# Attention scores on one Trainium2 core: minus the maximum enters through a row of ones in the masked keys

## The chip, the cores and the metric

The kernel runs on one core of one Trainium2 chip. The metric is the device time of one execution in microseconds; the time before is the median of 3 runs, 216.88 us (215.86 to 217.13). A lower time is better.

## What is computed

A block of a Flamingo-like network on 16 tiles of 128 x 256 float32: normalise x along its last axis, cross attention with 8 heads against `ctx` (queries from x, keys and values both `ctx`), then a gated feed-forward part. Cut to what matters:

```python
def _L0_xattn_ref(q, k, v, gamma):        # q: 16 x 128 x 256, k = v = ctx
    qh = q.reshape(B, 8, 16, 256)
    kh = k.reshape(B, 8, 16, 256)
    vh = v.reshape(B, 8, 16, 256)
    qk = jnp.einsum('bhdq,bhdl->bhql', qh, kh) * scale
    sm = jax.nn.softmax(qk, axis=-1)
    ret = jnp.einsum('bhql,bhdl->bhdq', sm, vh)
    return gamma * ret.reshape(B, 128, 256)
...
x = x + jnp.tanh(g_xattn[0]) * _L0_xattn_ref(_layernorm(x), ctx, ctx, gamma)
x = x + jnp.tanh(g_ffn[0]) * _L0_ffn_ref(_layernorm(x), ...)   # silu(gate) * up, then down
```

The weights of the feed-forward part are rounded to float8_e4m3 values first. The softmax is computed with its row maximum subtracted.

## The kernel before

There are 16 batches (`NB`). In a batch the 128 partitions are 8 heads of 16 rows, in 4 row groups of 32 partitions (`NG`); a row group holds two heads (`PAR`). Scores are made twice.

- **s fills** (`scores(n)`): per batch 8, one for each row group g and half t of the queries. A matmul of 32 rows takes the normalised queries `qn` as weights and the masked keys `km` (two copies of the keys, each with the rows of one head of the pair kept) as moving data, and fills a PSUM bank 128 x 512. VectorE takes minus the maximum of each half (`reduce_max`).
- **turn** (`turn(b)`): TensorE transposes the maxima of batch b (split in two bf16 parts by VectorE, `split_max`) and `ctx` into one bank; ScalarE copies the first half to `max_t` (`max_out`) and the second to `v_t` (`v_out`).
- **t fills** (`scores_t(n)`): the scores again, transposed: weights `c_sb`, moving data the masked queries `qm` (512 columns, float32), then two bf16 matmuls of 4 rows add minus the maximum from `max_t`. ScalarE takes the exponential of the bank (`exps`).
- **weighted** (`weighted(b)`): 16 matmuls of `p_t` with `v_t`.

A float32 matmul appears in the trace as two rows, and a full round of four fills in four different row groups runs side by side.

The order on every engine is written out by hand. TensorE first runs s fills 0 to 11, turn(0) and s fills 12 to 14; then, in **block b** (b = 0 to 15, with n = 8b and m = 8b + 15): s(m), t(n), s(m+1), s(m+2), t(n+1) to t(n+4), s(m+3), s(m+4), weighted(b-1), turn(b+1), s(m+5), t(n+5), s(m+6), t(n+6), s(m+7), t(n+7). So the third item of block b, s(m+1), is the first s fill of batch b+2, and the second, t(n), the first t fill of batch b. Each engine's queue is in order: what stands behind a waiting instruction waits too. The PSUM banks go round in a ring of 8.

GpSimd (POOL) makes, in its iteration b: at b = 2, 6 and 10 the reciprocal standard deviations of four batches (`pow_group`); `keys(b+2)`, two instructions for the masked keys; `queries(b+2)`, one for `qn` and two for the masked queries `qm`; then, at b = 2, 3, 5, 6, 7 and 8, `rounded` (two instructions over 128 x 768 for the rounding of weights), at b = 9 and 13 `attention` (two over 128 x 1024), at b = 12 `rstd_chunk(0)` and `norm_apply_first`. `keys(b+2)` waits until the maxima of batch b are taken.

Of the kernel before, what the change touches and what calls it, by code (L numbers as in the profile page):

```python
# [66 lines left out]
def build(nc, x, ctx, g_xattn, g_ffn, gamma, gate_w, up_w, down_w, gate_scale, up_scale, down_scale, out):  # L67
# [7 lines left out]
    with es:  # L75
# [26 lines left out]
        km = sb("km", [P, 2, PAR, L])  # L102
        qn = sb("qn", [P, 2, L])
        qm = sb("qm", [P, 4, PAR, L])
        neg_max = sb("neg_max", [P, 2, FILLS * PAR, 2])
        nm_parts = sb("nm_parts", [P, LT, P], bf16)
        max_t = sb("max_t", [P, 2, L], bf16)
# [777 lines left out]
```

## Time and profile before

| | |
|---|---|
| median of 3 runs | 216.88 us (215.86 to 217.13) |
| the profiled execution | 216.79 us, of which the span on the core 215.0 us |
| busy: TensorE / VectorE / ScalarE / GpSimd | 195.8 / 158.5 / 124.9 / 145.9 us |
| turn(1) ends / turn(15) ends | 22.7 / 124.6 us |
| attention part (blocks 0 to 15) | about 15 to 143 us; then the feed-forward part |

Matmuls are pipelined and their ends are modelled, so a busy TensorE is not one at its peak. In the rows below the engines are PE (TensorE matmul), PEld (its weight loads), DVE (VectorE), ACT (ScalarE), POOL (GpSimd); L715 is line 715 of the kernel before; times are microseconds from the start of the span.

### The profile page before, as it was taken

How to read it: one execution, taken by the hardware profiler on the slowest of the kernel's cores; microseconds unless marked ns; L12 is line 12 of the kernel's file. 1: busy time of each engine (PE TensorE's matmuls, PEld its weight loads, DVE VectorE, ACT ScalarE, POOL GpSimd, SP SyncE). 2: the span in 40 equal slices, each digit the busy share in tenths (PEclk: the TensorE clock that was granted, in tenths of full speed). 3: DMA queues.
4: the chain of work that ended last, by engine and by line, in shares of the span. 5: the costliest groups of instructions: out<-in, count | busy, mean ns of one | idle time of the engine just before them, and what ended most of it. 6: DMA issues, size and time to landing. Idle time of an engine off the chain costs nothing.

```text
span 215.0 us, 4666 instructions
## 1 busy us (share of the span) xinstructions
PE 195.8 (91%) x1760; PEld 117.6 (55%) x1760; DVE 158.5 (74%) x331; ACT 124.9 (58%) x241; POOL 145.9 (68%) x167
## 2 busy tenths in 40 slices
PE   0759999999999999999999988999799999999980
PEld 0225456665665566556655642447466766666670
DVE  3599999998999897679965633056956677674954
ACT  2013657876787578767875853369447545844430
POOL 5992889948999999965799003554554999566430
PEclk9988999999999999999999996999999999999997
DMA  5699601101131231232311412111320002002022
GB/s 181 198 351 386 132 2 52 39 24 41 52 112 58 84 107 38 68 93 64 115 46 51 132 38 82 50 48 53 104 101 0 2 0 98 3 0 98 5 98 98
DMA packets 19783, 17.75 MB, mean 83 GB/s; under 512 B 4016, under 2 KB 19248, under 8 KB 19760
## 3 DMA queue, kind: packets, MB, share of 16 engines
q1 hardware_dynamic: 19760, 17.44, 26.1%
q8 instruction: 14, 0.23, 0.5%
q14 instruction: 9, 0.07, 0.1%
HBM read 11.02 MB, written 6.42 MB: 81 GB/s over the span
## 4 chain that ended last, share of the span: by engine, by line
PE 77%; DVE 11%; issue 3%; ACT 3%; POOL 2%; DMA 1%; POOLq 1%; SPq 0%; DVEq 0%; ACTq 0%
PE ps L715 19%; PE ps L779 17%; PE ps L756 14%; PE ps L727 11%; PE ps L836 8%; DVE neg_max L534 6%; PE ps L730 4%; PE ps L743 1%; PE ps L740 1%; ACT p_t L459 1%; DMA c_sb<-in_ctx 1%; PE ps L766 1%; ACT xn L488 1%; DVE p_t L688 1%; POOLq L75 1%
## 5 line engine op out<-in xcount | busy, mean ns | idle before, releaser
L534 DVE TENSOR_REDUCE neg_max<-ps 128x2 f32<-128x512 f32 x128 | 79.3, 681 | 12.3 <-PE ps L715 12.2
L715 PE MATMUL ps<-km,qn 32*128 32x512 f32 x256 | 74.0, 669 | 8.5 <-POOL qn L342 7.7
L459 ACT ACTIVATE p_t<-ps 128x512 f32<-128x512 f32 x128 | 67.1, 600 | 21.4 <-PE ps L730 19.4
L727 PE MATMUL ps<-qm,c_sb 32*128 32x512 f32 x256 | 73.6, 635 | 1.3 <-ACT p_t L459 1.3
L779 PE MATMUL ps<-w_exp,w_gu 128*128 128x512 f16 x192 | 47.0, 390 | 1.3 <-DVE w_exp L585 1.3
L425 POOL TENSOR_TENSOR f_lo<-fu,f_hi 128x512 fp32r<-128x512 f32 x23 | 29.3, 1277 | 23.7 <-ACT f_hi L477 23.7
L730 PE MATMUL ps<-max_t,sel 4*128 4x256 bf16 x256 | 34.7, 268 | 0.0
L715 PEld LDWEIGHTS ps<-km,qn 32*128 32x128 f32 x256 | 25.2, 197 | 14.5 <-issue 14.1
L650 DVE SCALAR_TENSOR_TENSOR ga<-th,ps 128x512 f32<-128x512 f32 x24 | 16.4, 682 | 22.1 <-ACT th L472 22.1
L756 PE MATMUL ps<-p_t,v_t 128*32 128x256 f32 x512 | 30.9, 382 | 0.4 <-ACT p_t L459 0.4
L730 PEld LDWEIGHTS ps<-max_t,sel 4*128 4x128 bf16 x256 | 18.6, 94 | 22.8 <-issue 20.1
L472 ACT ACTIVATE th<-ps,gs_half 128x512 f32<-128x512 f32 x24 | 16.5, 686 | 24.0 <-PE ps L779 22.4
L727 PEld LDWEIGHTS ps<-qm,c_sb 32*128 32x128 f32 x256 | 26.8, 184 | 6.0 <-issue 3.5
L779 PEld LDWEIGHTS ps<-w_exp,w_gu 128*128 128x128 f16 x192 | 17.5, 100 | 21.8 <-issue 2.5
L836 PE MATMUL ps<-wd,f_hi 128*128 128x256 f32 x96 | 27.8, 324 | 0.7 <-POOL f_lo L425 0.7
L335 POOL TENSOR_SCALAR km<-c_sb,mask 128x256 f32<-128x256 f32 x32 | 14.9, 479 | 14.4 <-DVE neg_max L534 12.6
L836 PE MATMUL ps<-wd,f_lo 128*128 128x256 f32 x96 | 23.8, 281 | 0.0
L756 PEld LDWEIGHTS ps<-p_t,v_t 128*32 128x32 f32 x512 | 15.0, 109 | 13.5 <-ACT p_t L459 5.1
L836 PEld LDWEIGHTS ps<-wd,f_hi 128*128 128x128 f32 x96 | 18.1, 189 | 3.8 <-POOL f_lo L425 1.4
L342 POOL TENSOR_SCALAR qn<-x_sb,mv,rstd 128x256 f32<-128x256 f32 x16 | 19.8, 1236 | 0.2
L655 DVE SCALAR_TENSOR_TENSOR fu<-ps,gus,ga 128x512 f32<-128x512 f32 x24 | 18.0, 751 | 2.5 <-POOL f_lo L425 1.7
L445 ACT CAST max_t<-ps 128x256 bf16<-128x256 f32 x16 | 6.0, 372 | 23.2 <-PE ps L743 23.2
(65 smaller groups left out, 217.8 us busy)
## 6 DMA issues: line engine op xcount, KB each, us to landing
u_scr<-u_sb SPq DMA_DIRECT2D x32, 128.0 KB
u_n<-u_scr SPq DMA_DIRECT2D x16, 128.0 KB
r_n<-r_scr SPq DMA_DIRECT2D x16, 128.0 KB
out_x<-p_t SPq DMA_DIRECT2D x16, 128.0 KB, 1.8
x_sb<-in_x SPq DMA_DIRECT2D x3, 512.0 KB, 8.9
c_sb<-in_ctx SPq DMA_DIRECT2D x3, 512.0 KB, 8.9
w_all<-in_L_ffn_gate_w SPq DMA_DIRECT2D x1, 768.0 KB, 9.2
w_all<-in_L_ffn_up_w SPq DMA_DIRECT2D x1, 768.0 KB, 9.8
```

Source lines behind the costliest of these rows:

```text
L342: nc.gpsimd.tensor_scalar(qn[:, b % 2, :], x_sb[:, b, :], mv[:, b, 0:1], rstd[:, b:b + 1], ALU.subtract, ALU.mult).then_inc(qn_ok, 1)
L425: nc.gpsimd.tensor_tensor(f_lo[:, it, :], fu[:, it % 2, :], f_hi[:, it, :].bitcast(f32), ALU.subtract).then_inc(fl_ok, 1)
L459: nc.scalar.activation(p_t[:, b % 2, i, :], ps[:, bank_of["t", n][0], :], ACT.Exp, scale=DH ** -0.5).then_inc(exp_ok, 1)
L472: nc.scalar.activation(th[:, it % 2, :], ps[:, gate_bank(n, 0), :], ACT.Tanh, scale=gs_half[:, it:it + 1]).then_inc(th_ok, 1)
L534: nc.vector.tensor_reduce(neg_max[:, b % 2, at:at + PAR, 0], ps[:, bank_of["s", n][0], :].rearrange("p (e l) -> p e l", e=PAR), axis=AX.X, ...
L655: nc.vector.scalar_tensor_tensor(fu[:, it % 2, :], ps[:, gate_bank(n, 1), :], gus[:, it:it + 1], ga[:, it % 2, :], ALU.mult, ALU.mult).the ...
L715: nc.tensor.matmul(ps[:, bank, :], qn[rows, b % 2, P * t:P * (t + 1)], km[rows, b % 2].rearrange("p e l -> p (e l)"), start=True, stop=Tru ...
L727: nc.tensor.matmul(ps[:, bank, :], c_sb[rows, b, P * t:P * (t + 1)], qm[rows, b % 4].rearrange("p e l -> p (e l)"), start=True, stop=False)
L730: last = nc.tensor.matmul(ps[:, bank, L * e:L * (e + 1)], sel[head, e, :], max_t[head, b % 2, :], start=False, stop=(e == PAR - 1))
L756: last = nc.tensor.matmul(ps[SLOTW * g:SLOTW * (g + 1), bank, L * e:L * (e + 1)], v_t[:, b % 3, t, PAR * g + e, :], p_t[:, b % 2, i, L * e ...
L779: last = nc.tensor.matmul(ps[:, gate_bank(n, m), :], w[:, ht, P * it:P * (it + 1)], x_t[:, c, part, ht, :], start=(j == 0), stop=(j == 2 * ...
L836: last = nc.tensor.matmul(ps[:, PS_Y + q // 2, L * (q % 2):L * (q % 2 + 1)], f[:, it, P * q:P * (q + 1)], wd[:, it, :], start=(it == 0 and ...
```

## The change

Minus the maximum no longer enters the t fills by matmuls of its own.

- `km` is built as keys x mask + `one`, where `one` holds 1 in the first row of the other head of the pair; it has 4 buffers instead of 2 and is now also the weight of the t fills, whose `c_sb` matmul of 512 columns and two bf16 matmuls of 256 become two float32 matmuls of 256 columns.
- The maxima stay float32: `split_max` is gone, `reduce_max` writes into `nm`, and `turn` transposes that.
- `max_out` is two ScalarE instructions, one for each head of the pair, with the mask as scale.
- `queries` makes `qn` only. A new GpSimd step, `shifted_queries(b)`, adds `qn` and `max_t` to give `qm`; it waits for `max_out(b)`. In GpSimd's iteration b it is done for batch b+1, behind `keys(b+2)` and `queries(b+2)` and ahead of `rounded`.
- Subtracting the mean becomes adding its negative (`neg_m`, one small instruction for each group of batches).
- The second instruction of `binades` moves from VectorE to GpSimd, into `rounded`.

```diff
@@ gpsimd
             def keys(b):
-                pool.wait_ge(masks_ok, 1)
+                pool.wait_ge(masks_ok, 3)
                 pool.wait_ge(c_in[group_of(b)], 16)
-                if b >= 2:
-                    pool.wait_ge(max_ok, FILLS * (b - 1))
-                for e in range(PAR):
-                    nc.gpsimd.tensor_scalar(km[:, b % 2, e, :], c_sb[:, b, :], mask[:, e:e + 1], 1.0,
-                                            ALU.mult, ALU.mult).then_inc(k_ok, 1)
+                if b >= 4:
+                    pool.wait_ge(exp_ok, FILLS * (b - 3))
+                for s in range(PAR):
+                    nc.gpsimd.tensor_scalar(km[:, b % 4, s, :], c_sb[:, b, :], mask[:, 1 - s:2 - s], one[:, s:s + 1],
+                                            ALU.mult, ALU.add).then_inc(k_ok, 1)
 
             def queries(b):
                 pool.wait_ge(r1_ok, group_of(b) + 1)
...
+                nc.gpsimd.tensor_scalar(qn[:, b % 3, :], x_sb[:, b, :], neg_m[:, b:b + 1], rstd[:, b:b + 1],
+                                        ALU.add, ALU.mult).then_inc(qn_ok, 1)
+
+            def shifted_queries(b):
+                pool.wait_ge(mt_sb, PAR * (b + 1))
                 if b >= 2:
-                    pool.wait_ge(max_ok, FILLS * (b - 1))
-                nc.gpsimd.tensor_scalar(qn[:, b % 2, :], x_sb[:, b, :], mv[:, b, 0:1], rstd[:, b:b + 1],
-                                        ALU.subtract, ALU.mult).then_inc(qn_ok, 1)
-                if b >= 4:
-                    pool.wait_ge(exp_ok, FILLS * (b - 3))
+                    pool.wait_ge(exp_ok, FILLS * (b - 1))
                 pool.wait_ge(qn_ok, b + 1)
-                for e in range(PAR):
-                    nc.gpsimd.tensor_scalar(qm[:, b % 4, e, :], qn[:, b % 2, :], mask[:, e:e + 1], 1.0,
-                                            ALU.mult, ALU.mult).then_inc(qm_ok, 1)
+                q = qn[:, b % 3, :].rearrange("p (a l) -> p a l", a=1).broadcast_to([P, PAR, L])
+                nc.gpsimd.tensor_tensor(qm[:, b % 2], max_t[:, b % 2], q, ALU.add).then_inc(qm_ok, PAR)
...
                 pool.wait_ge(w_exp_ok, k + 1)
+                nc.gpsimd.tensor_scalar(exp, exp, E4M3_MIN_EXP, E4M3_MAGIC, ALU.max, ALU.mult).then_inc(w_mag, 1)
+                pool.wait_ge(w_mag, k + 1)
                 nc.gpsimd.tensor_tensor(raw, raw, exp, ALU.add).then_inc(w_sum, 1)
...
+            shifted_queries(0)
             for b in range(NB):
                 if b + 2 < NB:
                     if b + 2 in (2, 4, 8, 12) and group_of(b + 2) > 1:
                         pow_group(group_of(b + 2))
                     keys(b + 2)
                     queries(b + 2)
+                if b + 1 < NB:
+                    shifted_queries(b + 1)
                 if b in HALF_ROUNDED:
                     rounded(HALF_ROUNDED.index(b))
@@ scalar
             def max_out(b):
                 act.wait_ge(m_ok, b + 1)
                 if b >= 2:
-                    act.wait_ge(exp_ok, FILLS * (b - 1))
-                nc.scalar.copy(max_t[:, b % 2, :], ps[:, bank_of["T", b][0], 0:L]).then_inc(mt_sb, 1)
+                    act.wait_ge(qm_ok, PAR * (b - 1))
+                for e in range(PAR):
+                    nc.scalar.activation(max_t[:, b % 2, e, :], ps[:, bank_of["T", b][0], 0:L], ACT.Copy,
+                                         scale=mask[:, 1 - e:2 - e]).then_inc(mt_sb, 1)
@@ tensor
             def scores_t(n):
                 b, i = divmod(n, FILLS)
                 t, g = i // NG, (i + ASIDE) % NG
                 if i == 0:
-                    pe.wait_ge(mt_sb, b + 1)
                     pe.wait_ge(qm_ok, PAR * (b + 1))
                 bank, held = bank_of["t", n]
                 bank_free(held)
-                rows, head = slice(SLOTW * g, SLOTW * (g + 1)), slice(SLOTW * g, SLOTW * g + ROWS)
-                nc.tensor.matmul(ps[:, bank, :], c_sb[rows, b, P * t:P * (t + 1)],
-                                 qm[rows, b % 4].rearrange("p e l -> p (e l)"), start=True, stop=False)
+                rows = slice(SLOTW * g, SLOTW * (g + 1))
                 for e in range(PAR):
-                    last = nc.tensor.matmul(ps[:, bank, L * e:L * (e + 1)], sel[head, e, :], max_t[head, b % 2, :],
-                                            start=False, stop=(e == PAR - 1))
+                    last = nc.tensor.matmul(ps[:, bank, L * e:L * (e + 1)], km[rows, b % 4, 1 - e, P * t:P * (t + 1)],
+                                            qm[rows, b % 2, e, :], start=True, stop=True)
                 last.then_inc(st_ok[g], 1)
```

On GpSimd, in iteration 3 of the kernel before (keys and queries of batch 5, then the second half-matrix of the rounding), every instruction works for a batch that TensorE reaches later:

```order
L335 TENSOR_SCALAR km<-c_sb,mask 128x256 [waits max_ok,c_in2,masks_ok]
L335 TENSOR_SCALAR km<-c_sb,mask 128x256
L342 TENSOR_SCALAR qn<-x_sb,mv,rstd 128x256 [waits max_ok,r1_ok]
L348 TENSOR_SCALAR qm<-qn,mask 128x256 [waits qn_ok,exp_ok]
L348 TENSOR_SCALAR qm<-qn,mask 128x256
L367 TENSOR_TENSOR w_all<-w_all,w_exp 128x768 [waits w_exp_ok]
L369 TENSOR_TENSOR w_gu<-w_all,w_exp 128x768 [waits w_sum]
```

The same place in the changed kernel, from the shifted queries of batch 3 through `rounded` to the shifted queries of batch 4:

```order
L346 TENSOR_TENSOR qm<-max_t,qn 128x512 [waits exp_ok,qn_ok,mt_sb]
L363 TENSOR_SCALAR w_exp<-w_exp 128x768 [waits w_exp_ok]
L365 TENSOR_TENSOR w_all<-w_all,w_exp 128x768 [waits w_mag]
L367 TENSOR_TENSOR w_gu<-w_all,w_exp 128x768 [waits w_sum]
L330 TENSOR_SCALAR km<-c_sb,mask,one 128x256 [waits exp_ok,c_in2,masks_ok]
L330 TENSOR_SCALAR km<-c_sb,mask,one 128x256
L337 TENSOR_SCALAR qn<-x_sb,neg_m,rstd 128x256 [waits qm_ok,r1_ok]
L346 TENSOR_TENSOR qm<-max_t,qn 128x512 [waits exp_ok,qn_ok,mt_sb]
```

The masked queries have moved behind a wait for ScalarE's `max_t` (`mt_sb`), and the rounding and the next keys and queries stand behind that.

On TensorE, the start of block 2 of the kernel before, from block 2's first fill on:

```order
L715 MATMUL ps<-km,qn 128x512 [waits u_ok]
L727 MATMUL ps<-qm,c_sb 128x512 [waits mt_sb,vt_sb,qm_ok]
L730 MATMUL ps<-max_t,sel 128x256 x2
L715 MATMUL ps<-km,qn 128x512 [waits max_ok,qn_ok,k_ok]
L715 MATMUL ps<-km,qn 128x512 [waits exp_ok]
```

The same place in the changed kernel:

```order
L695 MATMUL ps<-km,qn 128x512 [waits u_ok]
L707 MATMUL ps<-qm,km 128x256 [waits vt_sb,mt_sb,qm_ok]
L707 MATMUL ps<-qm,km 128x256
L695 MATMUL ps<-km,qn 128x512 [waits max_ok,qn_ok,k_ok]
L695 MATMUL ps<-km,qn 128x512 [waits exp_ok]
```

The order of TensorE is the same; the first t fill of a batch still waits for `qm_ok`, and the s fill right behind it for `k_ok` and `qn_ok` of the batch two further on.

## Rows read from the trace of the kernel before

**Rows 1.** The page's chain that ended last, share of the span by engine.

```profile
PE 77%; DVE 11%; issue 3%; ACT 3%; POOL 2%; DMA 1%; POOLq 1%; SPq 0%; DVEq 0%; ACTq 0%
```

**Rows 2.** One 8 us window: length, busy PE, PEld, DVE, ACT, POOL, clock.

```profile
52.00:60.00 8.00, 8.00 (x94) 4.83 (x94) 7.42 (x15) 6.01 (x14) 7.65 (x8) 1.00 0.13 39
```

**Rows 3.** Timeline of PE over block 4: start us, length us, line, operation.

```profile
58.85 0.39 PE L743 MATMUL ps<-ident,c_sb 128*128 128x128 f32 x2
59.16 0.69 PE L715 MATMUL ps<-km,qn 32*128 32x512 f32 x1
...
60.14 0.69 PE L727 MATMUL ps<-qm,c_sb 32*128 32x512 f32 x1
...
60.35 0.80 PE L715 MATMUL ps<-km,qn 32*128 32x512 f32 x2
60.67 0.67 PE L727 MATMUL ps<-qm,c_sb 32*128 32x512 f32 x2
...
63.92 1.93 PE L756 MATMUL ps<-p_t,v_t 128*32 128x256 f32 x32
...
65.91 0.39 PE L743 MATMUL ps<-ident,c_sb 128*128 128x128 f32 x2
```

**Rows 4.** Timeline of ACT behind the turn of 58.85: start, length, line.

```profile
59.27 0.37 ACT L445 CAST max_t<-ps 128x256 bf16<-128x256 f32 x1 [1.22 <-PE ps L743]
59.54 0.40 ACT L452 COPY v_t<-ps 128x256 f32<-128x256 f32 x1
```

**Rows 5.** Groups by line and form: busy us, mean ns, idle before.

```profile
L342 POOL TENSOR_SCALAR qn<-x_sb,mv,rstd 128x256 f32<-128x256 f32 x16 | 19.8, 1236 | 0.2
L335 POOL TENSOR_SCALAR km<-c_sb,mask 128x256 f32<-128x256 f32 x32 | 14.9, 479 | 14.4 <-DVE neg_max L534 12.6 <-DMA c_sb<-in_ctx 1.5
L488 ACT ACTIVATE xn<-x_sb,shift,rstd 128x256 f32<-128x256 f32 x12 | 6.2, 592 | 1.1 <-POOL shift L388 1.1
L727 PEld LDWEIGHTS ps<-qm,c_sb 32*128 32x128 f32 x256 | 26.8, 184 | 6.0 <-issue 3.5 <-ACT p_t L459 1.1 <-DVE neg_max L534 0.6
```

**Rows 6.** Timelines of ACT and POOL, late in the attention part.

```profile
141.62 0.62 ACT L477 CAST f_hi<-fu 128x512 fp32r<-128x512 f32 x1
142.32 1.28 POOL L425 TENSOR_TENSOR f_lo<-fu,f_hi 128x512 fp32r<-128x512 f32 x1 [0.94 <-ACT f_hi L477]
```

**Rows 7.** Timelines of POOL and PE at the first s fill.

```profile
5.59 1.23 POOL L342 TENSOR_SCALAR qn<-x_sb,mv,rstd 128x256 f32<-128x256 f32 x1
6.97 3.79 PE L715 MATMUL ps<-km,qn 32*128 32x512 f32 x16 [6.97 <-POOL qn L342]
```

**Rows 8.** Timeline of POOL: pow_group, keys, rounded, keys; and an attention step.

```profile
56.46 0.24 POOL L325 TENSOR_SCALAR veps<-mv 128x4 f32<-128x4 f32 x1
...
57.91 0.93 POOL L335 TENSOR_SCALAR km<-c_sb,mask 128x256 f32<-128x256 f32 x2
...
61.41 1.80 POOL L367 TENSOR_TENSOR w_all<-w_all,w_exp 128x768 f32<-128x768 f32 x1
...
65.10 0.94 POOL L335 TENSOR_SCALAR km<-c_sb,mask 128x256 f32<-128x256 f32 x2
...
82.20 2.35 POOL L375 TENSOR_TENSOR u_n<-u_n,r_n 128x1024 f32<-128x1024 f32 x1
```

**Rows 9.** Windows of 2 us around a fall of the clock (columns as Rows 2).

```profile
126.00:128.00 2.00, 1.29 (x11) 0.98 (x12) 1.09 (x1) 1.43 (x3) 0.00 (x0) 1.00 0.15 37
132.00:134.00 2.00, 2.00 (x6) 0.60 (x4) 0.00 (x0) 0.00 (x0) 0.92 (x2) 0.50 0.36 119
```

**Rows 10.** Timeline of PE: eight matmuls at the lower and at the full clock.

```profile
130.85 3.53 PE L779 MATMUL ps<-w_exp,w_gu 128*128 128x512 f16 x8
...
138.75 1.90 PE L779 MATMUL ps<-w_exp,w_gu 128*128 128x512 f16 x8
```

**Rows 11.** Timeline of PE: the last matmuls of turn(1) and of turn(15).

```profile
22.29 0.39 PE L743 MATMUL ps<-ident,c_sb 128*128 128x128 f32 x2
...
124.16 0.39 PE L743 MATMUL ps<-ident,c_sb 128*128 128x128 f32 x2
```

More of the change, by code:

```diff
@@ L18 @@
 STEP = "stssttttssPTststst"
-ROWS = 4
 SLOTW = 32
@@ L99, in build @@
         c_sb = sb("c_sb", [P, NB, L])
[L102 to L107, printed above, removed]
+        km = sb("km", [P, 4, PAR, L])
+        qn = sb("qn", [P, 3, L])
+        qm = sb("qm", [P, 2, PAR, L])
+        nm = sb("nm", [P, 2, LT, P])
+        max_t = sb("max_t", [P, 2, PAR, L])
         p_t = sb("p_t", [P, 2, FILLS, PAR * L])
@@ L119, in build @@
         mv = sb("mv", [P, NB, 2])
+        neg_m = sb("neg_m", [P, NB])
         veps = sb("veps", [P, NB])
@@ L324, in pow_group @@
                 pool.wait_ge(ag1_ok, hi)
+                nc.gpsimd.tensor_scalar(neg_m[:, lo:hi], mv[:, lo:hi, 0], -1.0, None, ALU.mult)
                 nc.gpsimd.tensor_scalar(veps[:, lo:hi], mv[:, lo:hi, 1], EPS, None, ALU.add).then_inc(v1_ok, 1)
@@ L392, in norm_apply_first @@
                     q = t
-                    nc.gpsimd.tensor_scalar(xn2[:, q, :], x_sb[:, t, :], mv2[:, t, 0:1], rstd2[:, t:t + 1],
-                                            ALU.subtract, ALU.mult).then_inc(n2_ok, 1)
+                    nc.gpsimd.tensor_scalar(xn2[:, q, :], x_sb[:, t, :], neg_m2[:, t:t + 1], rstd2[:, t:t + 1],
+                                            ALU.add, ALU.mult).then_inc(n2_ok, 1)
+            shifted_queries(0)
             for b in range(NB):
@@ L532, in reduce_max @@
                 v.wait_ge(s_ok[g], n // NG + 1)
-                at = PAR * (NG * t + g)
-                nc.vector.tensor_reduce(neg_max[:, b % 2, at:at + PAR, 0],
+                if b >= 2:
+                    v.wait_ge(m_ok, b - 1)
+                to = nm[:, b % 2, t, :].rearrange("p (g s r) -> p g s r", g=NG, s=PAR)
+                nc.vector.tensor_reduce(to[:, g, :, 0],
                                         ps[:, bank_of["s", n][0], :].rearrange("p (e l) -> p e l", e=PAR),
                                         axis=AX.X, op=ALU.max, negate=True).then_inc(max_ok, 1)
-            def split_max(b):
-                v.wait_ge(max_ok, FILLS * (b + 1))
-                v.wait_ge(consts, 6)
-                if b:
-                    v.wait_ge(m_ok, b)
-                parts = nm_parts[:].rearrange("p t (g r) -> p (t g) r", g=NG)
-                high, low = (parts[:, :, r:ROWS:2] for r in range(2))
-                pair = neg_max[:, b % 2].rearrange("p (m e) r -> p m e r", e=PAR)
-                with nc.allow_low_precision(reason="the two bf16 parts add up to the float32 maximum"):
-                    nc.vector.tensor_reduce(high, pair[:, :, :, 0:1], axis=AX.X, op=ALU.max).then_inc(mx_hi, 1)
-                v.wait_ge(mx_hi, 2 * b + 1)
-                nc.vector.tensor_reduce(pair[:, :, :, 1], parts[:, :, 0:ROWS].rearrange("p m (e r) -> p m e r", r=2)[:, :, :, 0:1],
-                                        axis=AX.X, op=ALU.max, negate=True).then_inc(mx_hi, 1)
-                v.wait_ge(mx_hi, 2 * b + 2)
-                with nc.allow_low_precision(reason="the two bf16 parts add up to the float32 maximum"):
-                    nc.vector.tensor_reduce(low, pair, axis=AX.X, op=ALU.add).then_inc(mx_ok, 1)
             def binades(k):
@@ L714, in scores @@
                 rows = slice(SLOTW * g, SLOTW * (g + 1))
[L715 to L716 removed]
+                nc.tensor.matmul(ps[:, bank, :], qn[rows, b % 3, P * t:P * (t + 1)],
+                                 km[rows, b % 4].rearrange("p e l -> p (e l)"), start=True, stop=True).then_inc(s_ok[g], 1)
             def scores_t(n):
```

58 lines of the change are left out of this document (20 added, 38 removed).

## The prediction

> **What bounds the kernel now.** I read first the chain that ended last [rows 1]: TensorE has 77% of it, no other engine above 11%. Then the windows of the attention part: in [rows 2] TensorE is busy the whole 8 us, VectorE 7.42, GpSimd 7.65, ScalarE 6.01. Then one block in the timeline of TensorE [rows 3]: the last matmuls of one turn start at 58.85, those of the next at 65.91, so a block takes 7.06 us, and nothing in it stands still for long. GpSimd is nearly as full, but it works ahead: its keys and masked queries are for a batch that TensorE reaches a block later, so nobody waits for it. What the reader should take from this: before, the only thing between a turn and the t fills that need it is one ScalarE copy of 0.37 us [rows 4], and that is hidden: the first t fill of the new batch can start only when the round before it has passed its row group, at about 60.7 (the row of 60.67 holds two), 1.5 us behind the end of the turn (58.85 + 0.39 = 59.24).
>
> **What the change takes off TensorE.** The two bf16 matmuls of a t fill. A row group with an s fill hands over after 60.14 - 59.16 = 0.98 us [rows 3], one with a t fill at 60.35, 0.2 later. The new t fill has the same float32 columns in four shorter rows instead of two. A short row of 256 columns costs 1.93 / 8 = 0.24 us in `weighted` (32 rows in 8 rounds of four), so a t fill is 4 x 0.24 = 0.96: I take 0.98, like an s fill. Two t fills for each row group and block: 0.4 us less work a block, 6 us over 15 blocks, if TensorE stayed the bound. VectorE loses `split_max` and half of `binades`: it waits for TensorE already, so that gives nothing beyond the first blocks.
>
> **What it adds: a serial chain.** Two waits matter, and they follow from the two orders. In block b+1 the t fill of batch b+1 needs `shifted_queries(b+1)`, which needs turn(b+1), made at the end of block b. The s fill right behind it is the first of batch b+3 and needs `keys(b+3)` and `queries(b+3)`. GpSimd has these behind `shifted_queries(b+1)` and behind `rounded(b)`. TensorE is in order, so it can't go on to weighted and turn(b+2) before they are done, and GpSimd can't start `shifted_queries(b+2)` before turn(b+2). Nothing in this loop overlaps. From the end of a turn, step by step:
>
> - ScalarE starts 0.03 later (59.24 to 59.27) [rows 3, 4]. Two instructions, 0.27 apart (59.27, 59.54). One of this kind is not in the trace: the copies of 128x256 take 0.37, the activation of 128x256 with scale and bias from SBUF 0.59 [rows 5]. I take 0.46 and 0.36 apart; together 0.82, done at 0.85. Bounds 0.67 and 1.1.
> - GpSimd follows ScalarE 0.08 later, and a two-input instruction of 128x512 takes 1.28 (141.62 + 0.62 = 142.24, start 142.32) [rows 6]: 2.2.
> - `keys` twice and `queries` once. New forms, with two scalars from memory. The nearest rows: mult, mult with one such scalar 0.479; subtract, mult with two 1.236 [rows 5]. They differ in two things, the scalars and the subtraction, and the change keeps the first and drops the second. I take 0.47 each, 1.4 together, since the instruction reads one input tensor either way and only the operation could call for other code; if it's the two scalars, it is 3.7 (a rival below). Done at 3.65.
> - TensorE starts 0.15 later (5.59 + 1.23 = 6.82, start 6.97) [rows 7]: 3.8.
> - Eight fills are left ahead of weighted (the t fill with `qm` ran during the wait), two for each row group: 2 x 0.98, and 0.1 until all groups are through: 5.85.
> - weighted and turn 2.38 together (63.92 to 65.91 + 0.39) [rows 3]; two of the turn's four matmuls are now float32, an estimate of 0.02 more: 8.25.
>
> So a plain block takes **8.25 us** instead of 7.06: the TensorE work saved doesn't show. The PSUM ring doesn't add to it: VectorE and ScalarE have caught up in the wait.
>
> For keys and queries the Trainium skill has a figure too (GPSIMD Engine Reference, section 3.1): a body of up to two operations an element runs at 1.03 cycles an element, which at 1.2 GHz is 0.22 us for 256. The keys row agrees (0.479 [rows 5] less the 0.24 of a 4-element instruction [rows 8] leaves 0.24); the queries row, of two operations as well, is four times off, and the row decides there. By the page alone the three would cost 1.4 and the sum would stay.
>
> **What else stands in the loop.** Everything GpSimd does between `shifted_queries` and the keys:
>
> - `rounded`, behind iterations 2, 3, 5, 6, 7, 8. The two old instructions 3.69 (61.41 to 65.10) [rows 8]. The new one, 128x768: the keys' 0.479 is 0.24 as any small instruction has [rows 8] and 0.24 for 256 elements; three times the latter and the former once is 0.96 (at the rate of the 1.236 row it would be 3.2; max and mult with constants is closest to the keys row). With a wait of 0.08, 4.75 each, times 6: **28.5**.
> - `pow_group` at iterations 2, 6, 10: 56.46 to 57.91, 1.45, and `neg_m` 0.24 with its gap: 1.75, times 3: **5.2**.
> - `attention(0)`: two of 2.35 [rows 8] and gaps, **4.85**. `attention(1)` is behind batch 14, where no keys follow: hidden.
> - `rstd_chunk(0)` and `norm_apply_first`: 1.45 + 0.5, and 4 x 0.46 for the same form as the queries: **3.8**.
>
> Blocks 1 to 13 then take 13 x 8.25 + 42.4 = 149.7 us. Block 14 has no keys and no s fills: 2.2 + 0.15 + 2.06 + 2.4 = 6.8. Turn(1) ended at 22.68 [rows 11]; the first fill comes 0.5 earlier (queries 0.75 shorter, `neg_m` 0.24 longer) and VectorE's chain is shorter by `split_max`, an estimate of 0.5: I put it at 21.7. Turn(15): 21.7 + 149.7 + 6.8 = 178.2 against 124.55: **+53.6 us**. Behind turn(15) the work is as before.
>
> **The clock.** After 126 to 128, in which TensorE was busy 1.29 of 2 us, and a like stretch behind it, the granted clock was 0.50, 1.2 GHz, in 132 to 134 [rows 9], and eight matmuls took 3.53 us where 1.90 is their time at 2.4 GHz [rows 10]: 1.63 lost by one fall. In the eight blocks with 4 us or more in the loop TensorE stands still over 5 us. I expect a fall in each, at 1.3 us on average (between 0 and 1.63, nearer the upper end since the work resumes at once): **+10.4**.
>
> Sum, against the profiled execution's 216.79 (span 215.0 and 1.8 around it; 0.1 below the median): 216.8 + 53.6 + 10.4 = 280.8, **281 us**.
>
> **The rivals.**
>
> 1. *The form with two scalars is slow* (1.22 whatever the operation). For: the queries row. Against: nothing tells scalars from subtraction. A block takes 2.25 more, 13 times, 29; the norm 3 more; 313, and 318 if the clock also falls in plain blocks. 20%.
> 2. *Only the new instruction of `rounded` is slow* (3.2 instead of 0.96): 6 x 2.2 = 13 more, 294. 7%.
> 3. *The weight loads of the short rows aren't hidden.* A t fill then takes 4 x (0.24 + 0.184) = 1.7 instead of 0.98, with the load of [rows 5]; one t fill for each row group lies in the loop: 0.7 x 14, 10 more, 291. Against it: the s fills of today load twice too, and two rows of 512 columns with both loads take no more than 0.98; weighted's 0.24 holds its loads as well. 8%. That is what the Trainium skill would give (TensorE: Matmul & The Clock Gate, Part 3): "LDWEIGHTS overlaps with in-flight MATMULs only when row_grp differs", and here four rows in turn use one row group.
> 4. *Not slower:* keys and shifted queries are there when TensorE asks, and the 0.4 us a block is kept: 216.8 - 6, 211. It decides at the 1.5 us between the end of a turn and the first t fill: all of ScalarE's and GpSimd's steps would have to fit in it, where the shifted queries alone end at 2.2. 3%.
> 5. *Only the shifted queries are late*, the keys are somehow ahead: 2.2 + 0.15 - 1.5 - 0.4 = 0.45 a block, 15 blocks, 224. It would need another order on GpSimd than the one printed. 2%.
>
> The forecast itself has 60%, its own range 266 (no fall of the clock, quicker ScalarE) to 293 (each fall at its full price, ScalarE at 1.1). The range 264 to 316 adds rivals 2 and 3 and part of rival 1. A measurement of this kernel can tell about 1% from no change: slower by more than 1% in cases 1, 2, 3, 5 and the forecast, 96%; faster 3%; within 1% 1%.
>
> **What would show it.** Turns 8.2 us apart in plain blocks and 13 behind `rounded`; ScalarE's `max_t` ends 0.85 behind a turn; GpSimd waits longest for `max_t`, about 5.5 us in a plain block; TensorE's longest for `km` or `qn`, with an s fill, not a t fill, as the waiter; the clock at 0.5 behind long waits. Wrong would be: keys at 1.2 us (rival 1), t rounds of 1.7 us (rival 3), turns 7 us apart (rival 4), or TensorE waiting on `qm` alone (rival 5).

## The result: 309.4 us, 1.43 times the time before

The changed kernel takes 309.4 us at the median of 5 runs (309.18 to 311.77), the kernel before 217.12 (215.86 to 217.8); the ratio is 1.428, 95% interval 1.421 to 1.434. The profiled execution is the one of 311.8 us, span 310.0. Some executions of every kernel here take a few per cent longer at a lower granted clock; every ratio below leaves those out.

Its page, busy tenths and granted clock in 40 slices of 7.75 us:

```profile
PE   1889793664991673909284699939889989999992
PEclk9877968595976595857667588778999999999998
```

TensorE stands still again and again up to slice 29, which is the attention part, and its clock is low just behind. The feed-forward part behind it takes about as long as before. What the engines waited for (us in total, times, the longest):

```profile
DVE nm L539 <- PE ps L695: 119.0, 41, 10.9
POOL qm L346 <- issue: 104.1, 14, 8.5
...
PEld ps L695 <- POOL km L330: 66.4, 14, 9.3
PE ps L695 <- POOL km L330: 58.8, 9, 8.9
```

L695 is the s fill, L330 the keys, L346 the shifted queries, L539 the maximum. TensorE waits for the keys in the s fills (9 times in its matmuls, 14 times in their weight loads), GpSimd waits for the turn ("issue" here: it starts as soon as ScalarE's two `max_t` are there, 0.14 us later), and VectorE and ScalarE wait for TensorE. That is the loop. Before, the largest waits of TensorE for GpSimd were in the first few microseconds [rows 7]. The groups that the sum was built on (busy us, mean ns), to be set beside [rows 5, 6, 8]:

```profile
L346 POOL TENSOR_TENSOR qm<-max_t,qn 128x512 f32<-128x512 f32 x16 | 20.3, 1267 | 111.0 <-issue 104.1
...
L447 ACT ACTIVATE max_t<-ps,mask 128x256 f32<-128x256 f32 x32 | 13.4, 471 | 33.3 <-PE ps L719 33.3
...
L330 POOL TENSOR_SCALAR km<-c_sb,mask,one 128x256 f32<-128x256 f32 x32 | 17.5, 558 | 2.0 <-DMA c_sb<-in_ctx 2.0
...
L363 POOL TENSOR_SCALAR w_exp<-w_exp 128x768 f32<-128x768 f32 x6 | 16.7, 2780 | 0.5
```

and, from the answer by form:

```profile
L337 POOL TENSOR_SCALAR qn<-x_sb,neg_m,rstd 128x256 f32<-128x256 f32 x16 | 8.9, 559 | 0.2
```

One turn of the loop, block 3, with `rounded` in it. First TensorE (start, length; L719 the turn, L732 weighted), then GpSimd:

```profile
42.55 2.84 PE L732 MATMUL ps<-p_t,v_t 128*32 128x256 f32 x32
...
45.60 0.38 PE L719 MATMUL ps<-ident,c_sb 128*128 128x128 f32 x2
...
48.32 1.13 PE L707 MATMUL ps<-qm,km 32*128 32x256 f32 x4
56.64 1.22 PE L695 MATMUL ps<-km,qn 32*128 32x512 f32 x2 [7.20 <-POOL km L330]
```

```profile
47.00 1.27 POOL L346 TENSOR_TENSOR qm<-max_t,qn 128x512 f32<-128x512 f32 x1 [8.43 <-issue]
48.35 2.81 POOL L363 TENSOR_SCALAR w_exp<-w_exp 128x768 f32<-128x768 f32 x1
51.24 1.80 POOL L365 TENSOR_TENSOR w_all<-w_all,w_exp 128x768 f32<-128x768 f32 x1
53.12 1.80 POOL L367 TENSOR_TENSOR w_gu<-w_all,w_exp 128x768 f16<-128x768 f32 x1
54.91 1.09 POOL L330 TENSOR_SCALAR km<-c_sb,mask,one 128x256 f32<-128x256 f32 x2
55.98 0.56 POOL L337 TENSOR_SCALAR qn<-x_sb,neg_m,rstd 128x256 f32<-128x256 f32 x1
```

The turn ends at 45.98; 1.02 later GpSimd starts and works without a gap until 56.54; the first t fill has long run (48.32), and 0.1 later the s fill starts. The turns of the whole attention part, worked out from the ends of their last matmuls, are these far apart (us; block b is counted here from the end of turn(b) to the end of turn(b+1), so `rounded` of iteration b stands in block b+1, and blocks 1, 5, 11 and 12 are the plain ones):

| block | 1 | 2 | 3 | 4 | 5 | 6 | 7 | 8 | 9 | 10 | 11 | 12 | 13 | 14 |
|---|---|---|---|---|---|---|---|---|---|---|---|---|---|---|
| before | 8.3 | 7.0 | 7.1 | 7.1 | 7.1 | 7.1 | 7.6 | 7.1 | 7.1 | 7.3 | 7.1 | 7.1 | 7.7 | 7.4 |
| after | 8.5 | 13.1 | 17.5 | 17.3 | 10.2 | 19.8 | 17.6 | 17.3 | 17.2 | 17.1 | 10.2 | 10.2 | 14.3 | 7.3 |

### The profile page after: what moved, and what is told of

Same layout as the page of the kernel before. It is cut to its first block and busy times, and to the rows that moved or that the text cites. A ratio compares the mean times of both kernels' runs of the same rounds, so it can differ in the third digit from the quotient of the medians.

```text
span 310.0 us, 4719 instructions
## 1 busy us (share of the span) xinstructions
PE 231.4 (75%) x1760; PEld 147.9 (48%) x1760; DVE 150.3 (48%) x276; ACT 133.0 (43%) x257; POOL 155.2 (50%) x159
## 5 line engine op out<-in xcount | busy, mean ns | idle before, releaser
L695 PE MATMUL ps<-km,qn 32*128 32x512 f32 x256 | 99.8, 865 | 67.9 <-POOL km L330 58.8
L539 DVE TENSOR_REDUCE nm<-ps 128x2 f32<-128x512 f32 x128 | 80.5, 685 | 119.1 <-PE ps L695 119.0
L707 PE MATMUL ps<-qm,km 32*128 32x256 f32 x512 | 103.0, 494 | 2.1 <-ACT p_t L462 1.8
L707 PEld LDWEIGHTS ps<-qm,km 32*128 32x128 f32 x512 | 67.5, 235 | 19.4 <-POOL qm L346 7.9
L346 POOL TENSOR_TENSOR qm<-max_t,qn 128x512 f32<-128x512 f32 x16 | 20.3, 1267 | 111.0 <-issue 104.1
L695 PEld LDWEIGHTS ps<-km,qn 32*128 32x128 f32 x256 | 30.2, 243 | 80.9 <-POOL km L330 66.4
L732 PE MATMUL ps<-p_t,v_t 128*32 128x256 f32 x512 | 35.6, 425 | 0.4 <-ACT p_t L462 0.4
L447 ACT ACTIVATE max_t<-ps,mask 128x256 f32<-128x256 f32 x32 | 13.4, 471 | 33.3 <-PE ps L719 33.3
L755 PEld LDWEIGHTS ps<-w_exp,w_gu 128*128 128x128 f16 x192 | 17.2, 98 | 21.0 <-DVE w_exp L570 1.5
L732 PEld LDWEIGHTS ps<-p_t,v_t 128*32 128x32 f32 x512 | 16.1, 124 | 21.9 <-ACT p_t L462 9.8
L330 POOL TENSOR_SCALAR km<-c_sb,mask,one 128x256 f32<-128x256 f32 x32 | 17.5, 558 | 2.0 <-DMA c_sb<-in_ctx 2.0
L811 PEld LDWEIGHTS ps<-wd,f_lo 128*128 128x128 f32 x96 | 18.3, 190 | 0.5
L363 POOL TENSOR_SCALAR w_exp<-w_exp 128x768 f32<-128x768 f32 x6 | 16.7, 2780 | 0.5
```

What stands on the lines that cost most here:

```text
L330: nc.gpsimd.tensor_scalar(km[:, b % 4, s, :], c_sb[:, b, :], mask[:, 1 - s:2 - s], one[:, s:s + 1], ALU.mult, ALU.add).then_inc(k_ok, 1)
L346: nc.gpsimd.tensor_tensor(qm[:, b % 2], max_t[:, b % 2], q, ALU.add).then_inc(qm_ok, PAR)
L363: nc.gpsimd.tensor_scalar(exp, exp, E4M3_MIN_EXP, E4M3_MAGIC, ALU.max, ALU.mult).then_inc(w_mag, 1)
L539: nc.vector.tensor_reduce(to[:, g, :, 0], ps[:, bank_of["s", n][0], :].rearrange("p (e l) -> p e l", e=PAR), axis=AX.X, op=ALU.max, negate ...
L695: nc.tensor.matmul(ps[:, bank, :], qn[rows, b % 3, P * t:P * (t + 1)], km[rows, b % 4].rearrange("p e l -> p (e l)"), start=True, stop=Tru ...
L707: last = nc.tensor.matmul(ps[:, bank, L * e:L * (e + 1)], km[rows, b % 4, 1 - e, P * t:P * (t + 1)], qm[rows, b % 2, e, :], start=True, st ...
```

## The experiments

All of them are edits of the changed kernel, but for three that are edits of the kernel before.

### What stands in the loop: e1_mag_on_vector, e2_keys_ahead, e4_both

The edit of e1 (the one of e4 has it too):

```diff
@@ gpsimd, rounded
-                nc.gpsimd.tensor_scalar(exp, exp, E4M3_MIN_EXP, E4M3_MAGIC, ALU.max, ALU.mult).then_inc(w_mag, 1)
-                pool.wait_ge(w_mag, k + 1)
@@ vector, binades
-                                        ALU.bitwise_and).then_inc(w_exp_ok, 1)
+                                        ALU.bitwise_and).then_inc(w_mag, 1)
+                v.wait_ge(w_mag, k + 1)
+                nc.vector.tensor_scalar(exp, exp, E4M3_MIN_EXP, E4M3_MAGIC,
+                                        ALU.max, ALU.mult).then_inc(w_exp_ok, 1)
```

> The changed kernel with the new first instruction of `rounded` (max, mult over 128x768) put back on VectorE; nothing else. Theory (what GpSimd does between the shifted queries and the next keys stands in the loop): that instruction took 2.78 us and its wait 0.08, six times, so 309.4 - 17 = 292, between 288 and 296 by how the clock falls. Rival (the time is TensorE's own, its shorter float32 rows and their loads): VectorE has room, nothing gets shorter, 309.

Measured: 298.1 us, ratio to before 1.375 (1.355 to 1.395). The blocks with `rounded` went from 17.3 to 14.1, so 3.2 each where 2.9 was expected, and turn(15) came at 203.4 instead of 221.8, 18.4 earlier. The total fell by 11 only: behind turn(15) the clock fell once more than in the changed kernel. The same eight matmuls of the first gate, in the profile of e1:

```profile
210.47 3.59 PE L756 MATMUL ps<-w_exp,w_gu 128*128 128x512 f16 x8
```

and in that of the changed kernel:

```profile
227.90 1.90 PE L755 MATMUL ps<-w_exp,w_gu 128*128 128x512 f16 x8
```

With the t fills and weighted beside it, that stretch cost e1 about 5 us. So the instruction is in the loop, at its full price; the total says so only when the clock is read too.

The edit of e2 (keys and queries one batch earlier; `km` with 4 buffers and `qn` with 3 have room for it):

```diff
+            keys(2)
+            queries(2)
             shifted_queries(0)
             for b in range(NB):
-                if b + 2 < NB:
-                    if b + 2 in (2, 4, 8, 12) and group_of(b + 2) > 1:
-                        pow_group(group_of(b + 2))
-                    keys(b + 2)
-                    queries(b + 2)
+                if b + 3 < NB:
+                    if b + 3 in (4, 8, 12):
+                        pow_group(group_of(b + 3))
+                    keys(b + 3)
+                    queries(b + 3)
```

> The changed kernel with keys and queries made one batch earlier on GpSimd (batch b+3 ahead of the shifted queries of b+1), so that they and `rounded` no longer stand between the shifted queries and the s fill that needs them. Theory: only the shifted queries are left in the loop. A plain block is 0.93 to the end of max_t and the wait, 1.27, 0.15, three rounds for one row group 3.0, weighted and turn 2.4: 7.8, and a block with `rounded` goes by GpSimd's own work, 1.27 + 6.5 + 1.65 = 9.4. With 21.5 to turn(1), 14 x 7.8 + 6 x 1.6 + 2 for the rest: turn(15) at 142, 234 in all (226 to 245), the clock at 1.00 in plain blocks. Rival (TensorE's own time): 309, since TensorE's work is the same. Rival (the latency of ScalarE and of the shifted queries alone makes it slow, the keys do not matter): above 290.

Measured: 239.1 us, ratio 1.103 (1.072 to 1.134). Plain blocks 7.7, turn(15) at 147.8. Both rivals fall: the same work on every engine, only issued in another order on GpSimd, takes 70 us less (part of it the clock: 0.938 over the span, 0.819 in the changed kernel). What the edit takes out of the loop is keys, queries and, with them, `rounded`. The blocks behind `rounded` were off one by one: every other one took 12.8 to 13.0, the rest 7.7, where 9.4 each was expected. In pairs that is 20.5 against 18.8; where the 1.7 lies wasn't looked into.

> Both edits: max and mult on VectorE, and keys and queries a batch earlier. Theory: `rounded` fits too (1.27 + 3.7 + 1.65 = 6.6 within 7.8), the loop through the shifted queries is all that is left: 14 x 7.8 behind 21.5, turn(15) at 131, 223 in all (219 to 229), still slower than before. Rival (TensorE's own time): 309 less nothing. Rival (with the keys ahead TensorE's saving shows at once): 211.

Measured: 224.3 us, ratio 1.035 (1.014 to 1.056); blocks of 7.8 us with or without `rounded`, turn(15) at 133.4. GpSimd in e4:

```profile
64.58 1.27 POOL L346 TENSOR_TENSOR qm<-max_t,qn 128x512 f32<-128x512 f32 x1 [3.08 <-issue]
65.81 1.82 POOL L363 TENSOR_TENSOR w_all<-w_all,w_exp 128x768 f32<-128x768 f32 x1
67.70 1.81 POOL L365 TENSOR_TENSOR w_gu<-w_all,w_exp 128x768 f16<-128x768 f32 x1
69.51 1.09 POOL L330 TENSOR_SCALAR km<-c_sb,mask,one 128x256 f32<-128x256 f32 x2
70.59 0.55 POOL L337 TENSOR_SCALAR qn<-x_sb,neg_m,rstd 128x256 f32<-128x256 f32 x1
72.34 1.29 POOL L346 TENSOR_TENSOR qm<-max_t,qn 128x512 f32<-128x512 f32 x1 [1.20 <-issue]
```

The same instructions as in block 3 of the changed kernel, but nobody waits for the last five; only the first is on the path, 7.76 us from one to the next. So the 85 us between e4 and the changed kernel are the work that stood behind the shifted queries, and what its waits did to the clock.

### What the clock cost: e3_warm_dummies, e7_one_dummy

The edit of e3; e7 has 1 in place of the 3:

```diff
                 scores_t(n)
+                if 0 < b < NB - 2:
+                    bank, held = bank_of["s", m + 1]
+                    bank_free(held)
+                    for _ in range(8 if b - 1 in HALF_ROUNDED or b in (10, 13) else 3):
+                        nc.tensor.matmul(ps[:, bank, :], ident[:], c_sb[:, b:b + 2, :].rearrange("p a l -> p (a l)"),
+                                         start=True, stop=True)
                 scores(m + 1)
```

> The changed kernel with matmuls that compute nothing of use (128x512 float32, into the bank that the next s fill overwrites) behind the first t fill of blocks 1 to 13: 3 in plain blocks, 8 in those behind `rounded`, `attention` and the norm, so that TensorE works while it would wait. Theory (the part beyond the forecast is mostly TensorE at 1.2 GHz behind its waits): the clock stays at 1.00, plain blocks take 8.5, the sum is 285 (281 to 290). Rival (the clock is not what it costs; the misses are other): 309 or, where dummies hold up the fills, more.

Measured: 299.4 us, ratio 1.381 (1.355 to 1.408). The mechanism held, the size didn't. A window of 16 us around block 3 (length, busy PE, PEld, DVE, ACT, POOL, then the clock), first of the changed kernel, then of e3:

```profile
46.00:62.00 16.00, 8.80 (x68) 5.80 (x72) 5.14 (x9) 5.83 (x12) 9.29 (x7) 0.68 0.05 16
```

```profile
46.00:62.00 16.00, 15.85 (x112) 8.86 (x113) 6.32 (x15) 6.27 (x14) 9.30 (x7) 1.00 0.06 17
```

Blocks behind `rounded` went from 17.3 to 15.2 us with work added and none removed. Weighted took 1.93 (it was 2.84 above). But in plain blocks the three matmuls last 2.84 us, longer than the wait they were to fill, and hold the s fill up: 10.7 instead of 10.2. Hence:

> The changed kernel with matmuls of no use in TensorE's wait, as in the run with dummies, but one instead of three in plain blocks, where the three (2.84 us) lasted longer than the wait. Theory (the rest of the miss is the clock): plain blocks go from 10.2 us to 8.6 to 8.9 at the full clock, those behind `rounded` stay at 15.2, the sum is 299.4 - 5 x 1.9 = 290 (287 to 294). Rival (the clock falls anyway, or isn't what costs): plain blocks of 10 us, 299 and more.

Measured: 291.6 us, ratio 1.343 (1.336 to 1.349), the clock at 0.986 over the whole span (0.819 in the profile of the changed kernel). Plain blocks 9.0 (expected 8.6 to 8.9), those behind `rounded` 15.2. Turn(15) came at 199.7, 22.1 earlier than in the changed kernel's profile, though TensorE does more. The dummies still cost e7 something: some 0.4 in each of the four plain blocks (9.0 against the 8.6 of the forecast's steps at their measured lengths, an estimate), and 2.3 in block 13, where keys and queries are done at 185.50 and the s fill starts at 187.87, behind eight dummies. So up to turn(15) the clock cost the changed kernel about 22.1 + 1.6 + 2.3 = 26 us, an estimate; 1.4 of it lies ahead of turn(1). The end of block 6 of e7, at clock 1.00:

```profile
94.22 0.70 PE L695 MATMUL ps<-km,qn 32*128 32x512 f32 x2 [1.88 <-POOL km L330]
...
96.25 1.93 PE L732 MATMUL ps<-p_t,v_t 128*32 128x256 f32 x32
...
98.39 0.38 PE L719 MATMUL ps<-ident,c_sb 128*128 128x128 f32 x2
```

The eight fills behind the wait take 2.03 us.

### Which form is slow on GpSimd: e8_mult_then_max

```diff
-                nc.gpsimd.tensor_scalar(exp, exp, E4M3_MIN_EXP, E4M3_MAGIC, ALU.max, ALU.mult).then_inc(w_mag, 1)
+                nc.gpsimd.tensor_scalar(exp, exp, E4M3_MAGIC, E4M3_MIN_EXP * E4M3_MAGIC, ALU.mult, ALU.max).then_inc(w_mag, 1)
```

> The changed kernel with the new GpSimd instruction of `rounded` written as mult, then max (the constants changed to match) instead of max, then mult; nothing else. Theory A (a form is slow when any of its two operations is something else than mult or add): 2.78 us as before, 309. Theory B (it is the first operation that decides): about 1.0 us, 6 x 1.8 less and up to a few us of clock with it, 294 to 300.

Measured: 310.2 us, ratio 1.428 (1.400 to 1.456). The instruction in e8, by form:

```profile
L363 POOL TENSOR_SCALAR w_exp<-w_exp 128x768 f32<-128x768 f32 x6 | 16.7, 2782 | 0.5
```

2.78 us as before: theory B falls, the order of the two operations doesn't matter. What is fast and what is slow fits theory A in all six forms that were timed: mult, mult 0.479 [rows 5], mult, add 0.558 and add, mult 0.559 with two scalars from memory, against subtract, mult 1.236 [rows 5] and max, mult or mult, max 2.78 for three times the elements. It is a rule from six forms, not more.

### Whether TensorE saved anything: e5, e6, e9 to e12

In e4 only the latency from the turn to the shifted queries was left. e5 hides it behind weighted:

```diff
-STEP = "stssttttssPTststst"
+STEP = "stssttttssTPststst"
...
-                if b > 0:
-                    weighted(b - 1)
                 if b + 1 < NB:
                     turn(b + 1)
+                if b > 0:
+                    weighted(b - 1)
```

> Keys and queries a batch earlier and max, mult on VectorE (as the run with both edits, 7.75 us a block), and turn(b+1) put ahead of weighted(b-1) on TensorE, so that weighted covers ScalarE's and GpSimd's steps. Theory (all that is left is the latency from the turn to the shifted queries, 2.3 us, and TensorE's saving is real): blocks of 6.6 to 6.9 us at the full clock, 14 x 0.9 us less than 224, 209 to 213: faster than the kernel before. Rival (TensorE's saving is not real; the short float32 rows cost what the bf16 matmuls did): blocks of 7.06, 216 to 218. Rival (ScalarE, whose max_out then stands behind the exponentials, becomes the bound): 7.2 or more a block, 219 and up.

Measured: 219.0 us at the median, ratio 1.0067 (1.0027 to 1.0107). Blocks of 7.2 us, turn(15) at 125.4. It is neither the gain of the theory nor a loss by latency. The figures are those of the second rival (7.2 or more, 219 and up), but its reason isn't there: ScalarE isn't full, it waits for TensorE three times in a block, 0.61, 0.49 and 0.39 us (the first two):

```profile
46.59 0.59 ACT L469 COPY u_sb<-ps 128x512 f32<-128x512 f32 x1 [0.61 <-PE ps L735]
47.67 2.06 ACT L462 ACTIVATE p_t<-ps 128x512 f32<-128x512 f32 x4 [0.49 <-PE ps L710]
```

Where the 0.15 us beyond 7.06 lie can be read from TensorE, first in e5, then in the kernel before:

```profile
44.59 1.93 PE L735 MATMUL ps<-p_t,v_t 128*32 128x256 f32 x32
46.46 0.69 PE L698 MATMUL ps<-km,qn 32*128 32x512 f32 x1
...
51.21 0.44 PE L720 MATMUL ps<-ident,nm 128*128 128x128 f32 x2
...
51.80 1.93 PE L735 MATMUL ps<-p_t,v_t 128*32 128x256 f32 x32
```

```profile
45.04 0.69 PE L715 MATMUL ps<-km,qn 32*128 32x512 f32 x1
...
49.79 1.93 PE L756 MATMUL ps<-p_t,v_t 128*32 128x256 f32 x32
51.66 0.29 PE L740 MATMUL ps<-ident_b,nm_parts 128*128 128x128 bf16 x2
...
52.10 0.69 PE L715 MATMUL ps<-km,qn 32*128 32x512 f32 x1
```

The fills take 4.75 in both and weighted 1.87 in both. The turn, with its maxima in float32, takes 0.59 until the next matmul starts, where with bf16 parts it took 0.44. That is the whole difference. The control, the same edit in the kernel before:

> The kernel before with turn(b+1) ahead of weighted(b-1) and nothing else: the control for the run above. Theory: nothing waited for the turn before, so the block stays at 7.06 us and the time at 216 to 218. Rival (the earlier turn by itself makes blocks shorter): 7.0 or less, under 215.

Measured: 225.4 us at the median, ratio 1.029 (1.001 to 1.056). The profiled execution (226.0) has a stretch of low clock (0.77 in 70 to 80 us, 0.88 in 80 to 90) that lengthens its blocks 7 and 8; where the clock is 1.00 its blocks take 7.4 us, with 4.82 for the fills and 0.68 for the turn. In the kernel before, the earlier turn costs 0.3 a block; neither expectation foresaw that, and it wasn't followed up. It doesn't make the gain of e5 over e4.

Then the order of the fills, in e9 on top of e5, and in e10 in the kernel before (there with PT in place of TP); the diff is against the changed kernel, and the calls in the block are written in the same order:

```diff
-STEP = "stssttttssTPststst"
+STEP = "stststststTPststst"
```

> The version with keys ahead, max and mult on VectorE and the turn ahead of weighted (7.2 us a block, 217 to 219), with s and t fills strictly alternating on TensorE instead of four t fills in a row. Theory (what is left is the ring of 8 banks: eight maxima of 0.62 us each have to be taken while 16 fills run in 4.76 us, and a row of like fills makes one engine wait for the other): 4.3 to 4.6 us for the fills, blocks of 6.8 to 7.0, 211 to 214. Rival (VectorE's total of 5.0 and up to 2.2 more a block is the bound, whatever the order): 7.2 as before, 216 to 218.

> The kernel before with strictly alternating s and t fills and nothing else, the control for the run above. Theory: its t fills are 0.2 us longer and both of a row group's fills still follow each other, so 7.0 to 7.3 us a block, 215 to 220. Rival (the order alone does it): 211 to 214 here too.

Measured: e9 217.2 us, ratio 1.005 (1.000 to 1.010); blocks of 7.2, as its rival said. The rival's reason, VectorE's total, isn't it, though: from 110 to 120 us VectorE is busy only 6.12 of 10, and the blocks take 7.2 there too. e10: ratio 1.004 (0.998 to 1.009), no change in the time either; its blocks take 7.3, within what was expected. The last two runs took TensorE's work itself away. e11, from e9:

```diff
-                for e in range(PAR):
-                    last = nc.tensor.matmul(ps[:, bank, L * e:L * (e + 1)], km[rows, b % 4, 1 - e, P * t:P * (t + 1)],
-                                            qm[rows, b % 2, e, :], start=True, stop=True)
+                last = nc.tensor.matmul(ps[:, bank, :], km[rows, b % 4, 0, P * t:P * (t + 1)],
+                                        qm[rows, b % 2].rearrange("p e l -> p (e l)"), start=True, stop=True)
```

> The alternating version with each t fill as one float32 matmul of 512 columns with one pair of weight loads, instead of two of 256 with their own; the second head's mask is left out, so part of the scores is wrong and only the time is read. It asks why the bf16 matmuls' removal shows nowhere (16 fills take 4.76 us before and in the versions of after). Theory A (the short rows with their two more float32 loads eat the saving): the fills take 4.1 to 4.4 us, blocks 6.6 to 6.9, 208 to 213. Theory B (VectorE and the ring of banks set the pace of the fills): 4.76 us, 7.2 a block, 216 to 218.

Measured: 218.9 us, ratio 1.011 (1.003 to 1.020), blocks of 7.2. And e12, from the kernel before:

```diff
-                nc.tensor.matmul(ps[:, bank, :], c_sb[rows, b, P * t:P * (t + 1)],
-                                 qm[rows, b % 4].rearrange("p e l -> p (e l)"), start=True, stop=False)
-                for e in range(PAR):
-                    last = nc.tensor.matmul(ps[:, bank, L * e:L * (e + 1)], sel[head, e, :], max_t[head, b % 2, :],
-                                            start=False, stop=(e == PAR - 1))
+                last = nc.tensor.matmul(ps[:, bank, :], c_sb[rows, b, P * t:P * (t + 1)],
+                                        qm[rows, b % 4].rearrange("p e l -> p (e l)"), start=True, stop=True)
```

> The kernel before with the two bf16 matmuls of each t fill left out (the exponentials are then taken without the maximum; turn, max_out and split_max still run). The saving that the forecast took at 0.4 us a block, alone. Theory A (TensorE sets the pace): blocks of 6.5 to 6.7 us, 208 to 212. Theory B (VectorE and the ring set it): 7.0, 215 to 217.

Measured: 214.0 us, ratio 0.986 (0.982 to 0.990), and nearly all blocks of 7.06 us as before; from turn(1) to turn(15) it is 1.5 us shorter, all of it in blocks 1, 10, 13 and 14, but turn(1) comes 1.2 later, at a lower clock. So in the profiles turn(15) comes 0.3 us earlier, and the part behind it is 1.1 shorter; the rest of the 3 us isn't located. TensorE in e12, from the start of one block's fills to weighted, and the next:

```profile
102.52 0.69 PE L715 MATMUL ps<-km,qn 32*128 32x512 f32 x1
...
107.28 1.93 PE L753 MATMUL ps<-p_t,v_t 128*32 128x256 f32 x32
...
109.58 0.69 PE L715 MATMUL ps<-km,qn 32*128 32x512 f32 x1
```

Sixteen fills in 4.76 us, exactly as in the kernel before (59.16 to 63.92) [rows 3], though 16 bf16 matmuls are gone. In e11, which has no short rows and two weight loads for each t fill where e9 has four, the same 4.76 up to the turn, and beside it VectorE in one unbroken row of eight maxima:

```profile
105.98 0.69 PE L698 MATMUL ps<-km,qn 32*128 32x512 f32 x1
...
110.74 0.44 PE L719 MATMUL ps<-ident,nm 128*128 128x128 f32 x2
```

```profile
107.14 4.88 DVE L539 TENSOR_REDUCE nm<-ps 128x2 f32<-128x512 f32 x8 [0.87 <-PE ps L698]
```

Four contents of the t fills (the kernel before, e12, e5, e11), two orders of the fills (e5, e9) and two places of the turn give the same 4.76 us. Only the kernel before with its order changed takes more, 4.82 in e6 and 4.97 in e10. Four rounds at 0.98 a round, back to back, would be 3.9. So TensorE, busy by the page all the time, did not set the pace of the fills in the kernel before; what the bf16 matmuls took in a block of 7.06, it had to spare.

What sets it can be read in e11. The weight loads of its s fills waited for a maximum 39 times (waits, then the loads of one block; the first number of a row is the start):

```profile
PEld ps L698 <- DVE nm L539: 10.7, 39, 0.4
```

```profile
49.63 0.18 PEld L698 LDWEIGHTS ps<-km,qn 32*128 32x128 f32 x1 [0.21 <-DVE nm L539]
...
50.23 0.18 PEld L698 LDWEIGHTS ps<-km,qn 32*128 32x128 f32 x1 [0.30 <-DVE nm L539]
```

The next follows at 50.83. These s fills start 0.60 apart, and a maximum takes 0.61 (4.88 for eight): each fill takes a bank that a maximum has just freed. So in e11 the ring of eight banks behind VectorE sets the pace. That it does so in the kernel before as well is argued from the same 4.76 us, not shown: there hardly a load is marked as waiting for a maximum. A run with fewer or shorter maxima wasn't made.

## Why the prediction was right, and where it was off

The forecast was 281 us with a range of 264 to 316, slower with 96%; measured 309.4. The mechanism was right: the loop, the order of its steps and who waits for whom are those of the forecast. The size was less good. 309.4 lies above the forecast's own range of 266 to 293, held at 60%, and inside the wide one only because that had been stretched for rivals, most of all for rival 1, which did not come true. That the wide range held is in part luck: what filled it was rival 2 together with a clock that cost far more than forecast. Step by step:

- *The loop.* The weight loads of the s fill wait for the keys 14 times, 66.4 us in all; those of the t fills wait for the shifted queries 7.9 us in all. e2 takes the keys, and `rounded` ahead of them, out of the loop and gives 70 us back without changing any work.
- *The steps from the turn.* Forecast 0.93 to the start of the shifted queries, measured 1.02 (ScalarE's instruction 0.471 against 0.46). Shifted queries 1.27 (1.28). Two rounds 2.03 in e7 at clock 1.00 (2.05). Weighted and turn together 2.52 in e7 (96.25 to 98.77), forecast 2.40: the turn was forecast 0.02 longer than before and is some 0.14 longer. For a block behind `rounded` the forecast had 13.0 at the full clock; with the measured terms of this list it is 15.3, and e7 has 15.2.
- *Keys and queries.* 0.55 to 0.56 each, forecast 0.47: the quick form, so rival 1 is out. It was the subtraction that made the row of 1.236: with an addition in its place and both scalars still from memory it is 0.559. 0.26 for the three, 3.4 us in all.
- *rounded.* Here the named step failed: "three times the latter and the former once is 0.96". It took 2.78: rival 2, at 7%. 1.82 more, six times, 10.9 us. max with mult was put beside mult, mult because both have constants; the row that it was like is the one with subtract.
- *The clock* was the largest miss: 10.4 us forecast, about 25 measured. Turn(15) came 33.2 us later than the sum had it, of which 14.9 are left when the other terms of this list are taken off; 10.4 + 14.9 is 25.3. e7 gives nearly the same another way: 26 less the 1.4 ahead of turn(1) is 24.6. The step that failed is "in the eight blocks with 4 us or more": the clock fell in plain blocks too, and weighted and both rounds then ran low. A fall cost 2.1 us behind `rounded` (17.3 to 15.2 in e3), not 1.3.
- *The start.* Turn(0) came 0.5 us earlier, as forecast (14.9 against 15.4), but turn(1) at 24.4, not 21.7: 2.7 us, part of it the clock (0.66 from 20 to 30 us; e7, with 0.91 there, has turn(1) at 23.0). The forecast had also left out that the loop begins in block 0.
- *After turn(15)*: 88.2 us, before 90.4.

The sum again, against the profiled execution: 280.8 + 10.9 + 3.4 + 2.7 + 1.3 (ScalarE and its wait, 14 times 0.09) + 14.9 (clock) - 2.2 = 311.8. It closes by construction, since the 14.9 is a remainder; it also holds small misses such as the turn's 0.12 a block and block 14 (7.3, not 6.8). e7 is what supports it.

The first part of the prediction was wrong in one claim that didn't show in the number: "0.4 us less work a block, 6 us over 15 blocks, if TensorE stayed the bound". Rival 4's 211 us couldn't be had: with everything else repaired (e5, e9) the change is at best even with the kernel before, at 1.005 (1.000 to 1.010). e12 shows that TensorE's bf16 matmuls cost a block of 7.06 nothing, and e5 that the float32 turn costs each block 0.15. The chain of waits with 77% for TensorE [rows 1] had been read as a bound. Rival 3 is out by the rows: by it the eight fills in the loop would have taken 0.7 more than the 2.05 of the forecast, and they take 2.03 (e7).

No version here that keeps the maximum beats the kernel before; the one without it (e12) does, by 1.4%, but it takes the exponential unshifted.

## What to carry to other kernels

When a step moves behind a wait on an in-order engine, write down what stands between that step and the next thing anybody needs from the same engine; all of it is now in the loop, whatever cover it had. Issue what doesn't depend on the wait ahead of it: here one shift of two calls was worth 70 us, the clock that came back with it included. A saving on the engine with the largest share of the chain counts only once taking that work away is seen to shorten a block.
